# Layer 0 recurrence: whole turns of the angle on GpSimd in two operations per step, and a changed order of VectorE's work at a change of group

## The reference, cut to what matters

```python
x_val = z[..., :D].reshape(B, L, K, H)          # after projection and convolution, K = 32 heads of H = 32
p = exp(clip(score_scale * s_raw, -20, 20))
x5 = x_val[..., None]
phi = x5 * theta                                # M = 4 angles per channel
cos_b, sin_b = cos(phi), sin(phi)
poly = w[0] + w[1] * x5 - w[2] * square(x5)
cs = cumsum([p_w * poly * cos_b, p_w * poly * sin_b, p_w], axis=1)     # along the 2048 positions
re, im = num_re / den, num_im / den             # then root mean square norm per head
y = re_n @ W_re + im_n @ W_im                   # per head, 128 -> 32
return (y * silu(x_gate)) @ W_out
```

## Time and profile before

| | us |
|---|---|
| median of 3 runs | 2437.94 |
| lowest, highest of them | 2432.04, 2554.12 |
| the profiled execution, own time | 2441.48 |
| its span on the slowest core (core 5) | 2439.9 |
| spans of the 8 cores | 2418.9 to 2439.9 |

### The profile page before, as it was taken

How to read it: one execution, slowest core, us unless ns; L and a number is a source line. 1 busy time by engine, 2 the same in 40 slices (tenths; PEclk the granted TensorE clock), 3 DMA queues, 4 the chain that set the end, 5 groups by cost and what they waited for, 6 DMA issues and landing times.

```text
span 2439.9 us, 23103 instructions; the slowest of 8 cores (2418.9 to 2439.9 us)
## 1 busy us (share of the span) xinstructions
PE 1694.4 (69%) x7431; PEld 649.6 (27%) x7431; DVE 1416.3 (58%) x1689; ACT 1246.2 (51%) x1353; POOL 262.3 (11%) x276
## 2 busy tenths in 40 slices
PE   0157367776666775529999987986679947777774
PEld 0012122222222221214444432332553312122221
DVE  8787598988568988223332026145642386655442
ACT  1583388898678887311111123123445434668771
POOL 1000043333110000210000000000120000010001
PEclk9978676777666666859999999998559957899997
DMA  7552310111251100473220021011121120010001
GB/s 163 113 103 40 56 26 14 25 22 24 77 115 20 26 1 1 125 145 70 52 52 26 1 48 22 1 18 18 31 48 31 26 44 35 35 52 18 35 36 60
DMA packets 103694, 113.23 MB, mean 46 GB/s; under 512 B 80148, under 2 KB 80564, under 8 KB 101496
## 3 DMA queue, kind: packets, MB, share of 16 engines
q1 hardware_dynamic: 91192, 71.05, 11.3%
q0 software_dynamic: 12384, 40.69, 10.3%
HBM read 115.96 MB, written 16.81 MB: 54 GB/s over the span
## 4 chain that ended last, share of the span: by engine, by line
PE 41%; DVE 23%; ACT 17%; issue 12%; DMA 4%; POOL 1%; SPq 1%; DVEq 0%; ACTq 0%; POOLq 0%
PE PS L1338 9%; PE PS L1446 5%; PE PS L1379 5%; DVE cs L926 4%; ACT pt L1750 4%; PE PS L1776 3%; PE PS L1552 2%; PE PS L1811 2%; PE PS L790 2%; DVE rf L1786 2%; PE PS L1735 2%; DMA xres<-x 2%; DVE rt L1468 2%; PE PS L1485 2%; PE PS L821 2%
## 5 line engine op out<-in xcount | busy, mean ns | idle before, releaser
L1750 ACT ACTIVATE pt<-PS,negb 128x1024 bf16<-128x1024 f32 (+2 forms) x240 | 228.0, 1023 | 149.0 <-PE PS L1735 149.0
L1338 PE MATMUL PS<-xn_fm,wgu 128*128 128x512 bf16 x1024 | 223.7, 382 | 0.0
L956 PE MATMUL PS<-sq,bones 128*128 128x512 bf16 x256 | 101.3, 539 | 166.7 <-ACT sq L939 166.7
L1491 DVE TENSOR_REDUCE mx<-PS 16x1 f32<-16x1024 f32 x64 | 77.6, 1212 | 175.1 <-PE PS L1485 175.1
L790 PE MATMUL PS<-xn_fm,wz 128*128 128x512 bf16 x512 | 141.3, 439 | 29.4 <-SPq L111 26.3
L926 DVE TENSOR_TENSOR_SCAN cs<-vr,carr 128x1024 bf16<-128x1024 bf16 x64 | 148.9, 2368 | 0.0
L1348 ACT ACTIVATE rl<-PS 128x1024 bf16<-128x1024 f32 x32 | 32.8, 1024 | 224.2 <-PE PS L1338 218.3
L926 DVE TENSOR_TENSOR_SCAN cs<-vr 128x1024 bf16<-128x1024 bf16 x64 | 142.9, 2273 | 0.0
L1338 PEld LDWEIGHTS PS<-xn_fm,wgu 128*128 128x128 bf16 x1024 | 100.7, 98 | 122.5 <-issue 3.4
L939 ACT ACTIVATE sq<-cs 128x1024 bf16<-128x1024 bf16 x128 | 127.8, 1047 | 7.7 <-DVE cs L926 6.0
L1735 PE MATMUL PS<-RK,RV 64*128 64x512 bf16 (+3 forms) x640 | 96.5, 381 | 47.8 <-ACT pt L1750 45.3
(11 more groups left out here) (261 smaller groups left out, 3269.9 us busy)
## 6 DMA issues: line engine op xcount, KB each, us to landing
wz<-l_wz POOLq DMA_DIRECT2D x32, 384.0 KB, 5.4
xt<-x SPq DMA_DIRECT2D x8, 1024.0 KB, 7.0
xres<-x SPq DMA_DIRECT2D x16, 512.0 KB, 4.5
x<-sgt SPq DMA_DIRECT2D x16, 512.0 KB, 3.1
wgu<-l_wgu POOLq DMA_DIRECT2D x8, 1024.0 KB, 10.4
wp<-l_wproj POOLq DMA_DIRECT2D x32, 256.0 KB, 3.6
xo<-x SPq DMA_DIRECT2D x16, 512.0 KB, 3.9
out<-yo SPq DMA_DIRECT2D x16, 512.0 KB, 2.9
```

Source lines behind the costliest of these rows:

```text
L956: t = do("tensor", lambda e, _s=s2, _r=r: e.matmul(PM[:, _s * 512:(_s + 1) * 512], bones[:], sq[_r][k][:, _s * 512:(_s + 1) * 512], start= ...
L1338: g = (lambda e, _w=w, _f=f, _d=dc, _b=bb, _t=tt: e.matmul(PS[:, _b + _f * 512:_b + (_f + 1) * 512], _w[:, _d * 512 + _f * 128:_d * 512 + ...
L1750: e.activation(pt[_g][:, 0:_o], PS[:, _b:_b + _o], AF.Exp, bias=sb["negb2"][:, _h:_h + 1], scale=0.125))
```

## The change

`turn_1` moves from ScalarE to GpSimd and takes in `turn_2`, which leaves VectorE: GpSimd makes th * x + MAGIC in one `tensor_scalar` and subtracts MAGIC in a second, with a wait on its own first result between them. `turn_3` stays on VectorE and waits for GpSimd's second result. The tile `magic` and its fill are gone. In the loop `scan(s, 0, v0)` is moved up, ahead of `finish_y`: at a change of group VectorE's order becomes values 0, values 1, turn_3, scan 0, gr, yh, scan 1. On GpSimd's queue this puts the `carr` copy of scan 0 ahead of the two operations of `turn_1(s + 2)`, and that of scan 1 behind them.

```diff
-                          ("magic", (128, 1), F32),
...
-    do("vector", lambda e: e.memset(sb["magic"][:], MAGIC))
...
-        need("scalar", t_xv[it], t_abs.get(s - 2))
-        t_u[s] = do("scalar", lambda e: e.activation(
-            frac[s % 2][:], xv[b][:], AF.Identity, bias=sb["magic"][:, 0:1],
-            scale=th))
-
-    def turn_2(s):
-        need("vector", t_u[s])
-        return do("vector", lambda e: e.tensor_scalar(
+        need("gpsimd", t_xv[it], t_abs.get(s - 2))
+        t_u[s] = do("gpsimd", lambda e: e.tensor_scalar(
+            out=frac[s % 2][:], in0=xv[b][:], scalar1=th, scalar2=MAGIC,
+            op0=ALU.mult, op1=ALU.add))
+        need("gpsimd", t_u[s])
+        t_u[s] = do("gpsimd", lambda e: e.tensor_scalar(
             out=frac[s % 2][:], in0=frac[s % 2][:], scalar1=MAGIC, scalar2=None,
             op0=ALU.subtract))
 
-    def turn_3(s, t):
+    def turn_3(s):
...
-        need("vector", t)
+        need("vector", t_u[s])
...
         v0 = values(s, 0)
-        if nxt:
-            u = turn_2(s + 1)
         v1 = values(s, 1)
         if nxt:
-            turn_3(s + 1, u)
+            turn_3(s + 1)
+        scan(s, 0, v0)
         if m == 1 and it > 0:
             finish_y(it - 1)
...
         if s + 2 < NS:
             turn_1(s + 2)
-        scan(s, 0, v0)
         scan(s, 1, v1)
```

More of the change, by code:

```diff
@@ L1083, in emit_l0_attn @@
     turn_1(0)
-    turn_3(0, turn_2(0))
+    turn_3(0)
     sincos(0)
```

## The result

The changed kernel takes 2480.93 us (median of 4 runs, 2478.56 to 2483.69) against 2437.94 before: ratio 1.0181, 95% interval 1.0166 to 1.0196, so 43 us slower. The forecast was 2472, 34 us slower. In some executions, whatever the kernel, the cores of one die show a lower granted clock and the time is 2 to 5% longer; the times and ratios in this text leave those out.

What follows compares the result with a forecast made beforehand. VectorE was taken to set the recurrence's pace except in steps m = 1, where ScalarE's chain is the floor. 2441.5 plus 13.5 + 20.5 = 34 gave 2475.5, on the 3.5 lower median 2472 us; 8-in-10 range 2435 to 2560.

Steps and rivals of the forecast that it cites:

- The bound: Recurrence: VectorE sets the pace except in steps m = 1; busy 246.3 of 270 us, ScalarE 237.4.
- turn_2's 0.60: VectorE loses turn_2: 0.60 us in each step, 2.40 in an iteration.
- the floor: Steps m = 1: ScalarE's chain through the cosine keeps the next values 0 from beginning before 11.2 us.
- The holding: GpSimd operations reading SBUF take turns with VectorE's two-SBUF-input operations: 1.1 us each, ends 0.86 and 2.16.
- The low end of my bounds: Holding of 0.86 us per GpSimd operation, from the 512-element copy's row; total then +13 us.
- The duration: Each of GpSimd's two turn operations lasts 1.3 us, a fifth of the way from copy to two-input addition.
- my sum: First half +1.69 us an iteration, second +2.56; eight of each, 13.5 + 20.5 = +34 us.
- goes between values 0 and values 1: First half, steps m = 0 and 1: GpSimd's first operation gets in there; with the second, 2.36 us.
- rival A: GpSimd is kept out until VectorE stops at turn_3: 2.65 us stall every step, +86, 2524 us; chance 0.14.
- m = 2 of the first half: Turns start ready, one holding falls on poly's product: 11.13 - 0.60 + 1.1 = 11.63 us.
- The order at a change of group: Steps m = 1: scan 0 ahead of gr fills VectorE's 2.83 us of idle time, down to the 11.2 limit.
- two holdings and 0.16: First half, m = 0 and 1: operations behind scan 0's cast cost two holdings plus 0.16 waiting, 2.36 us.

Runs made afterwards that it cites:

- e10: e8 plus, in the first 28 steps, a third GpSimd tensor_scalar that reads a resident SBUF tile and writes an unused one: 2455.99 us, ratio 1.0116.
- e11: e8 plus, in the first 28 steps, a third GpSimd operation that only fills an unused tile: 2439.88 us, ratio 1.0036.
- e7: Changed kernel with GpSimd's second operation written as times 1.0 plus -MAGIC, still in place: 2453.33 us, ratio 1.0077.
- e1: Kernel before with only scan 0 moved ahead of gr and yh, turns left on ScalarE and VectorE: 2430.22 us, ratio 0.9983.
- e12: Kernel before with scan 0 moved ahead and, in steps m = 1 only, both turn operations on GpSimd (second multiply-add), waiting for scan 0: 2426.21 us, ratio 0.9969.
- e2: Changed kernel with scan 0 back behind turn_1, so only the turns move to GpSimd: 2475.81 us, ratio 1.0171.
- e3: Changed kernel with turn_1(s + 2) issued right before scan 0, ahead of its cast on GpSimd's queue: 2455.49 us, ratio 1.0091.
- e8: e3 with GpSimd's second operation written as times 1.0 plus -MAGIC, as in e7: 2450.46 us, ratio 1.0071.

## Why the prediction was right in sum, and where it wasn't

*The bound, turn_2's 0.60 and the floor.* Right. The step m = 3 of the first half came to 6.95 (forecast 6.79), m = 1 of the second to 11.29 (11.2). The second half's others were 8.50, 11.88 and 7.58 for m = 0, 2 and 3 (9.09, 12.62, 8.00).

*The holding.* Right in kind, shown by e10 against e11; too large in size: 0.67 to 0.84 where I took 1.1. The low end of my bounds, worked out from the copy, was the better value. It explains the second half: the five holdings that lengthen an iteration there measure 0.84, 0.77, 0.82, 0.67 and 0.68, together 3.8 where I had 5.5, and the iteration fell short by 1.7. They don't all fall where I had put them: in m = 0 both are on values 1 and turn_3, none on the scan, and in m = 1 there are two (949.94), hidden under the floor.

*The duration.* "1.3 of duration" for both is the term that failed: 1.11 and 2.77. I had tied duration and holding together by the copy's row; the second operation holds VectorE for no longer than the first and lasts 2.5 times as long. Where VectorE waits for the result, as in the first half, the duration counts. The two steps with a stall were to take 2.36 more than their own work (by its own terms 2.40, since 1.3 less 1.1 is 0.2, not 0.16; that is worth 0.6 us in all); the stall alone was 3.93, m = 0 lasted 10.79 against a forecast of 9.13 and m = 1 12.71 against 12.24. e7 confirms the term: with the second operation at 1.04 the first half is 12.7 us longer than before (my sum had 13.5) and m = 0 lasts 9.14.

*The step "goes between values 0 and values 1".* Wrong: in the first half the first operation was passed over there and ran when VectorE had stopped behind values 1 (issued at 418.89, over at 421.01, values 1 over at 420.10). That is rival A's mechanism in one place, worth about 0.6 in each of those steps. It had not decided all steps, as A's 2524 us needed: VectorE waited for GpSimd 25 times in the first half, not 63 in all. What decides at which boundary GpSimd gets in stays open.

*m = 2 of the first half* came to 12.55 against 11.63: the second operation, begun in m = 1, held values 0 of this step and was late for turn_3 by 0.69, again its length.

*The order at a change of group.* Its gain alone is 4 us by e1, since turn_1 on ScalarE and, in e12, TensorE's product for poly come next. Together with the turns on GpSimd it gains nothing (e2), since it puts the cast ahead of them in the first half; I had seen that order of the queue, and priced it at two holdings and 0.16.

*The first iteration and step 32.* The first half exceeded my sum by 32 us. The settled iterations, 43.00 against 39.79, make 3.2 each, 26 in eight. The rest lies where I had counted an iteration like the others: iteration 0 has no change of group, so there is no idle time to fill (33.5 us before, 39.5 after), and step 32, the first of the second half, still waits 3.9 us for operations that stood behind a cast (7.5 before, 12.4 after).

So the first half cost some 32 us more than I had, most of it by the duration, and the second some 18 less, by the holding. The total was near because these errors have opposite signs. That is luck: with the holding right (0.84) and the rest as forecast, my sum would have been about +11 us, not +34, against a measured 43.

## What to carry to other kernels

Give an operation on GpSimd two prices: how long VectorE is held (here 0.7 to 0.8 us for 1024 elements of one tile, for the form that lasts 1.1 us and for the one that lasts 2.8; 2.16 for the addition of two tiles in the earlier trace rows), and how long its result takes (1.0 to 3.6 us for the same elements, by form). Which one is paid is decided by what stands ahead of it on GpSimd's queue: one-column casts that wait for a scan, with two operations behind them, cost 22 us here by the ratios of the changed kernel and e3. Where holding can't be avoided, let it fall where VectorE idles.

## What the runs showed of the hardware that I had not expected

- GpSimd's tensor_scalar of 128x1024 f32 takes 1.04 to 1.11 us as multiply and add, 2.77 as a single addition or subtraction, 3.63 as subtract and add.
- The form of 2.77 us holds VectorE for 0.77 (turn_3, 1.28 to 2.05), less than a third of its duration.
- A GpSimd fill of 128x1024 f32 (0.95 us) holds no operation of VectorE with two SBUF inputs (no more are stretched in e11 than in e8); a tensor_scalar of the same shape does, for 0.84.
- An added operation that no other engine waits for made the first half shorter (e11 against e8: 301.5 against 314.0 us), by the timelines because it moves the holdings. The ratios of the whole kernel, 1.0036 and 1.0071, just overlap in their intervals.
